# Attention scores on four 64x64 tiles of TensorE: a two-layer cross-attention kernel on one core

## The reference

```
x = x + xattn0(layernorm(x), ctx)      # 16 heads of 64, 256 queries, 77 keys, 32 batches
x = x + ffn0(layernorm(x))             # silu(x Wg) * (x Wu), then Wd; hidden 768
x = x + xattn1(layernorm(x), ctx)
x = x + int8_matmul(layernorm(x))      # rows and columns quantised by their absolute maximum

xattn: q = x Wq, k = ctx Wk, v = ctx Wv
       attn = softmax(q k^T / 8, over the 77 keys);  out = (attn v) Wo + bo
```

## Time and profile before

| | us |
|---|---|
| median of three runs | 1615.76 |
| lowest, highest | 1608.71, 1623.88 |
| span of the profiled execution | 1612.4 |
| PE busy | 1554.2 (96%) |
| PE weight loads busy | 1438.8 (89%) |
| DVE busy | 1364.5 (85%) |
| ACT busy | 1371.5 (85%) |
| POOL busy | 1273.3 (79%) |

### The profile page before, as it was taken

The page is one execution under the profiler, slowest core; times in us unless marked ns, Lnnn a source line. Parts: engine busy times, 40 slices in busy tenths (PEclk is TensorE's granted clock), DMA queues, the critical chain, the costliest instruction groups (busy, mean ns, idle before and its releaser), DMA issues.

```text
span 1612.4 us, 74691 instructions
## 1 busy us (share of the span) xinstructions
PE 1554.2 (96%) x27282; PEld 1438.8 (89%) x27282; DVE 1364.5 (85%) x3522; ACT 1371.5 (85%) x5640; POOL 1273.3 (79%) x1893
## 2 busy tenths in 40 slices
PE   7989898999999999999999999999999999999996
PEld 4555578999999999999999999999999999999995
DVE  6767567888888888888888887888898988998886
ACT  6656588899899989998999988889999999999984
POOL 5100088899999898999998988788999999999984
PEclk9999999999999999999999999999999999999998
DMA  9997689887887777878778999899899899988996
GB/s 262 366 274 250 232 170 186 169 175 173 183 166 173 177 173 169 176 173 183 166 173 179 171 173 160 154 183 189 193 200 199 190 192 193 202 191 193 190 189 124
DMA packets 740024, 307.81 MB, mean 191 GB/s; under 512 B 629201, under 2 KB 725361, under 8 KB 737841
## 3 DMA queue, kind: packets, MB, share of 16 engines
q1 hardware_dynamic: 738049, 299.32, 85.0%
q0 software_dynamic: 1840, 6.82, 1.4%
HBM read 87.09 MB, written 65.54 MB: 95 GB/s over the span
## 4 chain that ended last, share of the span: by engine, by line
PE 33%; POOL 32%; issue 11%; DVE 6%; DMA 3%; ACT 2%; SPq 1%; POOLq 0%; ACTq 0%; DVEq 0%
PE psum L328 25%; POOL pr L1660 10%; POOL p L1665 8%; POOL p L1673 6%; PE psum L1225 4%; POOL rs L388 3%; POOL hT_l L1651 3%; PE psum L326 2%; DMA pT<-p 2%; DVE oT_l L357 1%; PE psum L319 1%; DVE x L1640 1%; POOL y L1702 1%; ACT ex L1371 1%; DMA x2T<-x 1%
## 5 line engine op out<-in xcount | busy, mean ns | idle before, releaser
L1371 ACT ACTIVATE ex<-psum,nmax 128x77 f32<-128x77 f32 x2048 | 638.3, 336 | 43.2 <-DVE nmax L1499 35.9
L1665 POOL TENSOR_TENSOR p<-pr,p 128x308 f16<-128x308 f32 x512 | 414.2, 809 | 39.9 <-ACT p L343 1.8
L1371 ACT ACTIVATION_READ_ACCUMULATOR ex<-psum,nmax 128x1 f32 x2048 | 444.7, 217 | 0.0
L1660 POOL TENSOR_TENSOR pr<-ex,rden 128x308 f32<-128x308 f32 x512 | 375.0, 732 | 55.2 <-DVE rden L1504 54.5
L328 PE MATMUL psum<-xT,wq_h 128*64 128x256 f16 x4064 | 349.0, 273 | 0.0
L1499 DVE TENSOR_REDUCE nmax<-psum 128x4 f32<-128x308 f32 x512 | 240.7, 470 | 57.7 <-PE psum L328 55.8
L328 PE MATMUL psum<-xT,wq_l 128*64 128x256 f16 x2032 | 284.5, 273 | 0.0
L1673 POOL CAST p<-pr 128x308 f16<-128x308 f32 x509 | 242.2, 476 | 43.9 <-DMA pT<-p 12.0
L328 PE MATMUL psum<-kb,qT_h 128*64 128x154 f16 x4096 | 262.0, 231 | 8.7 <-PEq L398 4.6
L328 PE MATMUL psum<-wo_h,oT_h 128*64 128x256 f16 x1792 | 251.8, 275 | 11.7 <-DVE oT_l L357 10.2
L328 PE MATMUL psum<-wo_l,oT_h 128*64 128x256 f16 x1792 | 250.5, 273 | 0.0
(11 more groups left out here) (164 smaller groups left out, 3490.8 us busy)
## 6 DMA issues: line engine op xcount, KB each, us to landing
keys<-ks SPq DMA_DIRECT2D x16, 1232.0 KB, 7.7
kb<-keys SPq DMA_DIRECT2D x256, 77.0 KB, 2.8
vb<-vals SPq DMA_DIRECT2D x128, 154.0 KB
vals<-vs SPq DMA_DIRECT2D x64, 256.0 KB, 4.0
x_pair<-in_x_dram SPq DMA_DIRECT2D x32, 256.0 KB, 2.9
pT<-p SPq DMA_TRANSPOSE x512, 3.3
x_res<-in_x_dram SPq DMA_DIRECT2D x32, 256.0 KB, 3.1
mid_x<-y SPq DMA_DIRECT2D x32, 256.0 KB, 2.4
```

The source lines that it names most:

```text
L1371: last = act.activation(ex[i][:, t, b, :], SC[:, t, b * NK:(b + 1) * NK], ACT.Exp, bias=nmax[i][:, t, b:b + 1], accum_out=den[i][:, t, b:b ...
L1660: pool.tensor_tensor(pr[:, t, :, :], ex[i][:, t, :, :], r, ALU.mult).then_inc(s_p, 1)
L1665: pool.tensor_tensor(d[:, t, 1, :, 0:NK], pr[:, t, :, :], d[:, t, 0, :, 0:NK], ALU.subtract).then_inc(s_pl, 1)
```

## The change

`scores` makes both query halves in one stretch at the start of the unit. Each instruction now takes 64 rows (one head) by 64 columns (64 queries) with the 77 key columns of that head alone, and four of them, one for each quarter of the array, stand in a row. Even heads (rows 0 to 63) go to PSUM bank 0 and odd heads to bank 1. Softmax works on banks as before, so its halves are now even and odd heads of all 256 queries. Since both banks are written in one stretch, `scores(k)` waits for the exponentials of both halves of unit `k - 1`: `after(pe, s_e, 2 * k)`. A semaphore increment (`s_sgo`) stands behind the waits. `pT` is laid out by heads, and `weigh_values` reads it accordingly. On DVE, `maxima` of half 1 goes up in the unit, and the reciprocals of half 1 of the unit before go ahead of `maxima` of half 0. ACT, POOL and SP keep their lists.

```diff
-        pT = [sb(f"pT_{i}", [P, 2 * HPU, NQ], F16) for i in range(UNITS)]
+        pT = [sb(f"pT_{i}", [P, 2, 2 * HPU, P], F16) for i in range(UNITS)]
...
-                    sp.dma_start_transpose(pT[v][:, :, t * P:(t + 1) * P],
-                                           p16[v % 2][:, t, :, :, :].rearrange("p r h k -> p (r h k)")).then_inc(
+                    sp.dma_start_transpose(pT[v][:, b, :, :],
+                                           p16[v % 2][:, b, :, :, :].rearrange("p r h k -> p (r h k)")).then_inc(
...
-                def scores(k, u, t, k_need, halved):
-                    if t == 0:
-                        pe.wait_ge(s_ql, k + 1)
-                        pe.wait_ge(s_kb[u // 2], k_need)
-                    after(pe, s_e, QT * (k - 1) + t + 1)
+                def scores(k, u, k_need):
+
+                    pe.wait_ge(s_ql, k + 1)
+                    pe.wait_ge(s_kb[u // 2], k_need)
+                    after(pe, s_e, 2 * k)
+                    pe.sem_inc(s_sgo, 1)
                     i = u % 2
-                    for a in range(PPU):
-                        o = SC[:, t, a * 2 * NK:(a + 1) * 2 * NK].rearrange("p (a k) -> p a k", k=NK)
-                        ts = slice(t * P, (t + 1) * P)
-                        for q, (w, part) in enumerate(((qT_h[i], 0), (qT_h[i], 1), (qT_l[i], 0))):
-                            last = product(pe, o, w[:, a, ts], kb[u // 2][:, :, part, u % 2 * PPU + a, :], halved,
-                                           start=(q == 0), stop=(q == 2))
-                    last.then_inc(s_s, 1)
+                    terms = ((qT_h[i], 0), (qT_h[i], 1), (qT_l[i], 0))
+                    for t in range(QT):
+                        for a in range(PPU):
+                            at = slice((t * PPU + a) * NK, (t * PPU + a + 1) * NK)
+                            for q, (w, part) in enumerate(terms):
+                                done = (t, a, q) == (QT - 1, PPU - 1, len(terms) - 1)
+                                for b in range(2):
+                                    rows = slice(b * DH, (b + 1) * DH)
+                                    for c in range(2):
+                                        last = pe.matmul(SC[c * DH:(c + 1) * DH, b, at],
+                                                         w[rows, a, t * P + c * DH:t * P + (c + 1) * DH],
+                                                         kb[u // 2][rows, b, part, u % 2 * PPU + a, :],
+                                                         start=(q == 0), stop=(q == len(terms) - 1))
+                                    if done:
+                                        last.then_inc(s_s, 1)
...
                         if lay[0] is not None:
-                            scores(n + u, u, 0, 32 * (h + 1), True)
+                            scores(n + u, u, 32 * (h + 1))
...
-                        if lay[0] is not None:
-                            scores(n + u, u, 1, 0, True)
...
+                        if lay[(u - 1) // UNITS] is not None:
+                            reciprocals(n + u - 1, (u - 1) % 2, 1)
                         if lay[0] is not None:
                             maxima(n + u, u % 2, 0)
...
+                        if lay[0] is not None:
+                            maxima(n + u, u % 2, 1)
...
-                        if lay[(u - 1) // UNITS] is not None:
-                            reciprocals(n + u - 1, (u - 1) % 2, 1)
...
-                        if lay[0] is not None:
-                            maxima(n + u, u % 2, 1)
```

More of the change, by code:

```diff
@@ L941, in xattn_ffn_kernel @@
         s_end = sem("s_end")
+        s_sgo = sem("s_sgo")
         s_s, s_m, s_e, s_r = sem("s_s"), sem("s_m"), sem("s_e"), sem("s_r")
@@ L1083, in store_late_values, with turn_probabilities @@
                                      vs[0:rows, part, t, :]).then_inc(s_sv[t], 16)
-                def turn_probabilities(k, v, t):
-                    if t == 0:
+                def turn_probabilities(k, v, b):
+                    if b == 0:
                         after(sp, s_pv, k - 3)
-                    sp.wait_ge(s_pl, QT * k + t + 1)
-                    sp.dma_start_transpose(pT[v][:, :, t * P:(t + 1) * P],
-                                           p16[v % 2][:, t, :, :, :].rearrange("p r h k -> p (r h k)")).then_inc(
+                    sp.wait_ge(s_pl, 2 * k + b + 1)
+                    sp.dma_start_transpose(pT[v][:, b, :, :],
+                                           p16[v % 2][:, b, :, :, :].rearrange("p r h k -> p (r h k)")).then_inc(
                                                s_pt[v], 16)
@@ L1183, in _ @@
             def _(pe):
-                def scores(k, u, t, k_need, halved):
-                    if t == 0:
-                        pe.wait_ge(s_ql, k + 1)
-                        pe.wait_ge(s_kb[u // 2], k_need)
-                    after(pe, s_e, QT * (k - 1) + t + 1)
-                    i = u % 2
-                    for a in range(PPU):
-                        o = SC[:, t, a * 2 * NK:(a + 1) * 2 * NK].rearrange("p (a k) -> p a k", k=NK)
-                        ts = slice(t * P, (t + 1) * P)
-                        for q, (w, part) in enumerate(((qT_h[i], 0), (qT_h[i], 1), (qT_l[i], 0))):
-                            last = product(pe, o, w[:, a, ts], kb[u // 2][:, :, part, u % 2 * PPU + a, :], halved,
-                                           start=(q == 0), stop=(q == 2))
-                    last.then_inc(s_s, 1)
+                def scores(k, u, k_need):
[3 more added lines that the diff above has]
+                    pe.sem_inc(s_sgo, 1)
+                    i = u % 2
+                    terms = ((qT_h[i], 0), (qT_h[i], 1), (qT_l[i], 0))
[13 more added lines that the diff above has]
+                                        last.then_inc(s_s, 1)
                 def project(k, u, l):
@@ L1224, in weigh_values @@
                                 c = (u % 2 * HPU + hd) * DH
-                                last = pe.matmul(o[b * DH:(b + 1) * DH, a, :], vb[u // 2][:, part, c:c + DH],
-                                                 pT[u][0:NK, pp * HPU + hd, :], start=(q == 0), stop=(q == 2))
+                                at = pp * HPU + a
+                                last = pe.matmul(o[b * DH:(b + 1) * DH, a, :].rearrange("p (t q) -> p t q", q=P),
+                                                 vb[u // 2][:, part, c:c + DH],
+                                                 pT[u][0:NK, b, at:at + PPU + 1:PPU, :], start=(q == 0), stop=(q == 2))
                     last.then_inc(s_pv, 1)
```

## The result

The changed kernel takes 1803.28 us (median of 4, 1799.24 to 1805.5) against 1612.24 (median of 4): ratio 1.119, 95% interval 1.114 to 1.124. The forecast was 1671, with a range up to 1732. The side was right, the size was not.

The account below looks back on a forecast made before the run. PE was taken to set the pace, ACT and POOL some 7 to 9% behind. Span 1612.4 + 46 (layer 1) + 9 (layer 0) = 1667; the median stands 3.4 above the span, so 1671 us, range 1630 to 1732.

Parts of the forecast that it names:

- Part 1: Scores on PE: 48 instructions of 77 columns in 12 quartets take 0.41 us a unit, saving 0.41.
- the load row: PE trace row: four weight loads within 0.03 us after a wait, taken to show that tiles and instructions don't block each other.
- the rule on issue gaps: Skill page's floor near 25 ns per matmul: a quartet 0.10 us, the stretch of scores 1.2, some 1820 us in all.
- Part 2: PE around the scores: a change of tiling costs 0.10 us, two a unit 0.20, leaving 0.21 saved a unit.
- the upper bound for the gain: PE's own work, if nothing else moved: 256 x 0.21 = 54 us less in all.
- Rivals 1 and 2: Scores: row tiles load in turn, 1728 us, chance 0.13; or instructions are the limit, about 1900 us, chance 0.07.
- rival 2: Scores: instructions are the limit, up to 1.2 us more, about 1900 us (1820 by the issue floor); chance 0.07.
- Part 3: Scores waiting for both halves' exponentials: layer 1 bodies 19.7 us against 18.08, +46 us; layer 0 25.0 against 24.73, +9.
- Rivals 3 and 4: Waits are absorbed, 1619 us, chance 0.10; or PE's saving counts and the coupling does not, 1562 us, chance 0.08.
- The rest costs nothing that shows.: Semaphore increment, `pT` transposes, `weigh_values` columns and the lists of ACT, POOL and SP: no added time.
- layer 0's +0.27: Layer 0 body: 25.0 us against 24.73, times 34 bodies of layer 0 and of the change of layers, +9 us.
- and I add 0.5: Unit 1 of layer 0: 0.5 us on ACT's 4.38 for DVE's later first `maxima`, giving 4.9 against 5.34.

Follow-up runs that it names:

- e13: e12 with, in unit 0, DVE's second `maxima` right after the first and ACT's second exponentials ahead of `normalise`: 1658.28 us, 1.029 of the kernel before.
- e1: The changed kernel with PE's hardware loop over layer 1 running one body a round in place of two: 1720.84 us, 1.071 of the kernel before.
- e2: The kernel before with PE's layer 1 loop running four bodies a round in place of two: 1642.3 us, 1.021 of the kernel before.
- e5: e1 with DVE's `reciprocals` and second `maxima` of a unit where they were before the change: 1705.67 us, 1.058 of the kernel before.
- e11: e5 with DVE making `hf` ahead of the first `maxima` in unit 2 of layer 0: 1687.47 us, 1.047 of the kernel before.
- e3: The kernel before, its 128 x 64 tiles kept, with both halves in one stretch, the shared wait and the changed DVE order: 1734.14 us, 1.079.
- e12: e11 with, in unit 1, queries and turned rows (layer 1) ahead of the scores and `oT_l` ahead of DVE's first `maxima`: 1643.45 us, 1.021.
- e6: e1 with the scores behind the queries in each unit, in unit 1 of layer 1 behind `turned_x` too: 1915.85 us, 1.190 of the kernel before.
- e7: e6 with `oT_l`, and in unit 2 of layer 0 `hf`, ahead of the first `maxima` on DVE: 1714.98 us, 1.066 of the kernel before.
- e8: e7 with the kernel before's 128 x 64 score instructions, query halves and loop of two bodies: 1709.34 us, 1.061 of the kernel before.

## Why the prediction was wrong in size

**Right.** Part 1 held in the main: 0.43 from the first to the last start of a stretch, 0.038 a quartet for 0.034, and the choice of the load row over the rule on issue gaps was right. The Trainium skill's floor near 25 ns a matmul ("TensorE: Matmul & The Clock Gate", Back-to-back issue gap) doesn't hold between different tiles: 48 matmuls with their loads start within 0.43 us, 0.009 each. Part 2 held: 0.09 measured, 0.10 taken. What a unit saves is smaller than both together gave: 0.14 for 0.21 (units 2 and 3 of layer 1, where nothing waits, went from 4.53 and 4.09 to 4.40 and 3.95), so that the upper bound for the gain was 36 us and not 54. Rivals 1 and 2 are out; that rival 2's 1820 lies within 17 us of the measured time is luck, as its mechanism isn't there. Part 3 held in layer 1: 19.7 forecast, 19.89 measured, every unit within 0.1. Rivals 3 and 4 fell where the prediction said: nothing came earlier in the chain to `nmr`, which starts 2.66 after the scores of unit 0 (1137.15) where it was 2.56. Even where the exponentials did come early (`e13`), other steps of DVE and ACT took their place.

**Wrong, first step: "The rest costs nothing that shows."** I listed semaphores, transposes and streamed columns there, but not the code. The change adds 24 matmuls and 24 loads a unit, 28% to a round of layer 1's loop, and the round is then loaded anew each time. That is 82 us (after against `e1`), and `e2` brings the same about in the old kernel. The sentence "PE's longest new idle stretch is 1.8 us" was therefore wrong as well, and with it the full clock that all terms took for granted. Nothing in the rows of before shows the code as a resource. The view of DMA queues of the kernel before shows it indirectly: instruction loading in straight code and none in the loops.

**Wrong, second step: layer 0's +0.27.** It was +1.99, 60 us over some 30 bodies. Of the 1.7 that I missed 1.0 is unit 2, for which I subtracted 0.21 from 7.71 without asking what the moved scores covered. They stood ahead of the second `down`; without them PE reaches it 0.4 earlier, and DVE reaches `hf`, which frees its bank, later. Half a microsecond is unit 1: "and I add 0.5" stood for a first `maxima` that comes later, and left out that the change puts the second `maxima` and the reciprocals ahead as well. With DVE's old order (`e5`) unit 1 takes the 4.9 of the forecast. `e11`, with both mended, has 6.23, 4.92, 7.53 and 6.57, the forecast's 6.1, 4.9, 7.5 and 6.5. So the forecast was sound for the wait and for PE, and failed on DVE's list. The price of both is 33 us (`e1` against `e11`).

**The sum.** The terms missed are 82 for the code, 51 for layer 0 (60 - 9) and 6 for layer 1 (29 x 0.19, of which 0.14 are the 2 x 0.07 that units 2 and 3 save less), 139. The forecast was 1671, from a median 7 us above that of `e1`'s session: 1671 - 7 + 139 = 1803. That it comes out to the microsecond is luck; the terms are good to some 5 us. By cause: of the 191 us over the kernel before, 125 are one stretch with one wait and DVE's new order (`e3`), less 13 for the tiles (`e1` against `e3`), plus 82 for the code. This leaves some 3 us to the spread between sessions.

**Open.** How the 2.3 us of each pair beyond the standstills divide between slower matmuls and waits that they hide: in the slow body only one wait of 0.92 is left where an undisturbed one has three. Not settled either: which step of ACT or DVE keeps `e12` 2% above the kernel before; its waits in layer 1 add up to 1.06 a body, for three different operands.

## What to carry to other kernels

Before adding instructions to a loop, count what one round holds on that engine and look at the instruction queue in the DMA view: no packets inside the loop mean that it fits. If it only just fits, a quarter more code can cost more than the work it saves, as here. Two halves with work between them are a pipeline; joining them to save matmuls gives this away, so price the work that stood between and what it covered on the other engines' lists first. When a wait is moved, look up which engine's list stands behind the new place: in `e6`, `e7`, `e8` and `e13` the stall came back there.

## What the hardware showed unasked

- A loop of 1360 matmuls and loads a round fetches no code. One of 1744 fetches 9 packets of 16 KB each round and stands still for 3.4 to 4.7 us at its start and 0.9 to 1.7 us once more, 2.4 us later. One of 2720 fetches 13 and stands still for 2.8 to 3.6 us (`e2`; at one round of five 1.4 more), so more packets don't mean a longer standstill.
- The granted clock stayed at 1.00 through waits of 1.33 us in layer 0 and 1.10 in layer 1. It went to 0.50 in the standstills of 3.4 us and more (here from 1411.37 to 1414.81), and it stayed there while PE was already fully busy again (window 1419 to 1421). In `e2` it did so at four of five standstills, those of 3.1 us and more, and not at one of 2.8. In `e6` waits of 2.51 us were enough in layer 0, but mostly at every second one (686.85, and not 656.95), so the length of a wait alone doesn't decide it.
- Four tiles of 64 x 64 take 77 columns in 0.038 us a quartet on average (0.036 from the third on), their four weight loads included. The four start within 0.01 of each other.
- A change between tiles of 64 and 128 rows costs some 0.09 in either direction: into the scores 0.20 lie between the last start of `weigh_values` (256 columns, 0.107) and the first quartet.
